# A four-layer graph kernel: the attention layer's weight passes read an fp8 copy of the adjacency, held for two pairs of tiles, in place of f32 chunks

## The reference

```python
# layer 0: attention in both signs
h = inp @ W;  Wh1 = h @ a[:F];  Wh2 = h @ a[F:]
e = leaky_relu(Wh1 + Wh2.T, 0.2)
attention = softmax(where(adj > 0, e, -1e12));  negative = -softmax(where(adj > 0, -e, -1e12))
x = x + elu(concat([attention @ inp, negative @ inp]) @ wtrans)
# layer 1: relu((d^-1/2 adj d^-1/2 @ h) @ W + b)     layer 2: relu(adj @ (h > 0) @ sign(W).T)
# layer 3: (1 - t) * (h @ W) + t * (adj @ (h @ W))
```

## Time and profile before

| | |
|---|---|
| timed runs, us | 1029.56, 1032.15, 1032.72 |
| profiled execution, us | 1028.39, of which the span 1026.8 |
| PE, DVE, ACT, POOL busy in the span | 95%, 74%, 45%, 7% |
| attention's steady part, one pair | 35.6 us stretch: PE 35.60, DVE 33.2, ACT 25.4 busy |
| DMA packets in all | 154.81 MB |

### The profile page before, as it was taken

One profiled execution on the slowest core, in us unless ns is written; L12 is line 12 of the kernel. 1 busy time (PEld: TensorE's weight loads), 2 busy tenths in 40 slices (PEclk: granted clock), 3 DMA queues, 4 the chain that ended last, 5 costly groups with the idle time before them and its releaser, 6 DMA issues.

```text
span 1026.8 us, 20940 instructions
## 1 busy us (share of the span) xinstructions
PE 974.0 (95%) x7549; PEld 708.5 (69%) x7549; DVE 760.9 (74%) x1143; ACT 457.7 (45%) x827; POOL 72.8 (7%) x148
## 2 busy tenths in 40 slices
PE   5778899999999999999999799999999999999996
PEld 4436588888888888888888355555568874555553
DVE  5468889999999999999997565555557775555553
ACT  3476676777677777767767322222220001111111
POOL 2000000000000000000031000000004320000000
PEclk7589899999999999999999899999999999999998
DMA  6044476666666666566664034544654445656661
GB/s 233 1 45 96 119 158 139 147 151 146 151 157 151 141 159 124 148 143 158 144 124 170 33 132 171 196 165 169 216 185 160 137 165 184 208 201 209 215 220 61
DMA packets 44045, 154.81 MB, mean 151 GB/s; under 512 B 5068, under 2 KB 25189, under 8 KB 43877
## 3 DMA queue, kind: packets, MB, share of 16 engines
q1 hardware_dynamic: 35285, 142.37, 40.7%
q0 software_dynamic: 7488, 11.08, 13.3%
q10 hardware_dynamic: 1232, 0.85, 0.3%
HBM read 173.02 MB, written 14.50 MB: 183 GB/s over the span
## 4 chain that ended last, share of the span: by engine, by line
PE 45%; DVE 31%; issue 12%; ACT 8%; DMA 2%; DVEq 1%; ACTq 0%; POOL 0%; POOLq 0%
PE f_ya L1247 35%; DVE f_wm L1428 9%; DVE f_gb L1429 7%; DVE f_s_mat L1432 6%; PE f_yb L1164 5%; ACT f_gb L953 4%; DVE f_s_mat L1437 2%; ACT f_s_mat L963 2%; PE f_ya L1135 1%; PE f_yb L1158 1%; DVE f_xs L1467 1%; DVE f_w_res L1465 1%; DVE f_yt_sb L1457 1%; DMA f_ident<-ident_dram 1%; DMA f_e_tile<-f_e_dram 1%
## 5 line engine op out<-in xcount | busy, mean ns | idle before, releaser
L1174 PE MATMUL f_ya<-f_x_mat,f_s_mat 128*128 128x257 f16 x2028 | 351.3, 272 | 4.8 <-DVE f_s_mat L1437 4.8
L1174 PE MATMUL f_yb<-f_x_mat,f_s_mat 128*128 128x257 f16 x2028 | 334.2, 273 | 0.0
L1247 PE MATMUL f_ya<-f_x_mat,f_a 128*128 128x512 f16 x1352 | 318.7, 382 | 4.7 <-DVE f_x_mat L1495 4.7
L1247 PEld LDWEIGHTS f_ya<-f_x_mat,f_a 128*128 128x128 fp8e4 x1352 | 132.2, 99 | 140.1 <-DVE f_x_mat L1495 5.2
L1174 PEld LDWEIGHTS f_yb<-f_x_mat,f_s_mat 128*128 128x128 f16 x2028 | 196.1, 97 | 28.7
L1174 PEld LDWEIGHTS f_ya<-f_x_mat,f_s_mat 128*128 128x128 f16 x2028 | 149.7, 97 | 23.8 <-issue 5.3
L953 ACT ACTIVATE f_gb<-f_e_tile,f_expc 128x256 f32<-128x256 f32 x338 | 139.8, 493 | 3.2 <-DVE f_s_mat L1437 2.3
L963 ACT ACTIVATE f_s_mat<-f_wm 128x1792 f16<-128x1792 f32 (+1 forms) x52 | 82.7, 1590 | 111.1 <-DVE f_wm L1428 104.8
L1177 PE MATMUL f_ya<-f_ones,f_a 128*128 128x1 f16 x676 | 111.8, 165 | 0.0
L1428 DVE TENSOR_TENSOR f_wm<-f_gb,f_a 128x1792 f32<-128x1792 f32 (+1 forms) x52 | 98.2, 1888 | 14.9 <-ACT f_gb L953 13.1
L1571 DVE SCALAR_TENSOR_TENSOR f_gb<-f_gb 128x1664 f32<-128x1664 f32 x52 | 98.0, 1886 | 11.9 <-DVE f_s_mat L1621 11.9
(11 more groups left out here) (138 smaller groups left out, 745.8 us busy)
## 6 DMA issues: line engine op xcount, KB each, us to landing
f_gb<-adj_dram SPq DMA_DIRECT2D x52, 832.0 KB, 4.9
f_a<-f_a_dram SPq DMA_DIRECT2D x39, 832.0 KB, 4.5
f_a<-adj_t_dram SPq DMA_DIRECT2D x26, 896.0 KB, 6.1
f_a<-adj_t_dram SPq DMA_DIRECT2D x26, 768.0 KB, 5.1
f_a<-adj_t_dram POOLq DMA_DIRECT2D x26, 224.0 KB, 5.8
f_a_dram<-f_a SPq DMA_DIRECT2D x26, 224.0 KB, 6.1
f_a<-adj_t_dram POOLq DMA_DIRECT2D x26, 192.0 KB, 4.6
f_a_dram<-f_a SPq DMA_DIRECT2D x26, 192.0 KB, 5.9
```

The source lines that it names most:

```text
L1174: return pe.matmul(bank[:, 0:F + 1], s_mat[:, j, side, i], x_mat[:, j, x_side, 0:F + 1], start=start, stop=stop)
L1247: return pe.matmul(bank_a[p][:, 0:W], a8_pair[:, r, at:at + P], x_layer[layer][:, j, 0:W], start=(j == 0), stop=(j == TILES - 1))
```

## The change

`a8` becomes two pairs deep, `[P, 2, TILES, HP]`, and DVE's two passes read it in place of `a32`. The buffer `a32`, its 52 loads on SP and their semaphores go. POOL's loads no longer wait for `et_done` (the scores); from pair 2 on they wait for PE and DVE to be through the same chunk two pairs before, and for its store. The later layers read their pairs from the same two buffers, which turns the parity `r0` round and splits what SP waits for at the hand-over.

```diff
-        a32 = sb("a32", [P, 2, CM * HP])
-        a8 = sb("a8", [P, TILES, HP], F8)
+        a8 = sb("a8", [P, 2, TILES, HP], F8)
-        a8_pair = a32[:].rearrange("p r c -> p (r c)").bitcast(F8)[:, 0:2 * TILES * HP].rearrange("p (r c) -> p r c", r=2)
+        a8_pair = a8[:].rearrange("p r j c -> p r (j c)")
...
-                def load_chunk(m, c):
-                    lo, hi = CHUNKS[c]
-                    sp.dma_start(blocks(a32, c), adj_t[bass.ds(m, 1), :, lo:hi, :].rearrange("a p j c -> p (a j) c"))\
-                      .then_inc(a_here[c % 2], 16)
...
                 def pair(m, r, k):
-                    start = isinstance(m, int) and m == 0
+                    if isinstance(m, int) and m == 0:
+                        wait(et_done, 2)
+                        sp.dma_start(e_dram, e_rows[:]).then_inc(e_stored, 16)
+                        wait(e_stored, 16)
+                        load_e(0, 0)
+                        load_e(1, 1)
                     for c in range(NC):
-                        n = NC * m + c
-                        if not (start and c < 2):
-                            wait(wp_done, n - 1)
-                        load_chunk(m, c)
...
-                        elif not start and c == 1 and not (isinstance(m, int) and m == PAIRS - 1):
+                        if c == 1 and not (isinstance(m, int) and m in (0, PAIRS - 1)):
                             wait(g_done, NC * m)
                             load_e(m + 1, 1 - r)
-                        if not (start and c < 2):
-                            store_a8(m if c >= 2 else m - 1, (c - 2) % NC)
+                        store_a8(m, r, k, c)
...
-                wait(wp_done, NC * PAIRS)
-                for c in range(NC):
-                    wait(a8_stored[c], 16 * PAIRS)
-                wait(lo_done, 2 * NC * PAIRS)
...
-                    r0 = layer % 2 ^ 1
+                    r0 = layer % 2
                     if layer > 1:
                         wait(mm_done[layer - 1], TILES - 2)
+                    else:
+                        for c in range(NC):
+                            wait(a8_stored[1, c], 16 * (PAIRS // 2))
                     load_pair(layer, 0, r0)
                     if layer > 1:
                         wait(mm_done[layer - 1], TILES)
+                    else:
+                        for c in range(NC):
+                            wait(a8_stored[0, c], 16 * (PAIRS // 2 + 1))
+                        wait(s_free, NC * PAIRS)
+                        wait(lo_done, 2 * NC * PAIRS)
                     load_pair(layer, 1, r0 ^ 1)
...
                 def load_a8(m, c):
-                    if not isinstance(m, int) or m > 0:
-                        g.wait_ge(s_free, NC * m + c - NC + 1)
+                    if m > 1:
+                        g.wait_ge(s_free, NC * (m - 2) + c + 1)
+                        g.wait_ge(wp_done, NC * (m - 2) + c + 1)
-                        g.wait_ge(a8_stored[c], 16 * m)
+                        g.wait_ge(a8_stored[m % 2, c], 16 * (m // 2))
-                    g.dma_start(a8[:, lo:hi, :], adj_t[m, :, lo:hi, :])\
+                    g.dma_start(a8[:, m % 2, lo:hi, :], adj_t[m, :, lo:hi, :])\
-                g.wait_ge(et_done, 2)
...
-                def produce(m, c):
+                def produce(m, r, k, c):
-                    v.wait_ge(a_here[c % 2], 16 * (2 * m + c // 2 + 1))
+                    v.wait_ge(a8_here[r, c], 16 * k + 16)
-                    v.tensor_tensor(part(wm, c), part(gb, c), part(a32, c), ALU.min).then_inc(wm_done, 1)
-                    v.scalar_tensor_tensor(part(gb, c), part(gb, c), 1.0, part(a32, c), ALU.max, ALU.mult).then_inc(wp_done, 1)
+                    v.tensor_tensor(part(wm, c), part(gb, c), a8_part(r, c), ALU.min).then_inc(wm_done, 1)
+                    v.scalar_tensor_tensor(part(gb, c), part(gb, c), 1.0, a8_part(r, c), ALU.max, ALU.mult).then_inc(wp_done, 1)
```

More of the change, by code:

```diff
@@ L618, in fast_program @@
         xlo = sem("xlo")
-        a_here = [sem(f"a_here{i}") for i in range(2)]
         e_here = [sem(f"e_here{i}") for i in range(2)]
-        a8_stored = [sem(f"a8_stored{c}") for c in range(NC)]
+        a8_stored = {(r, c): sem(f"a8_stored{r}{c}") for r in range(2) for c in range(NC)}
         g_done = sem("g_done")
@@ L627, in fast_program @@
         hp_done = sem("hp_done")
-        a8_here = [sem(f"a8_here{c}") for c in range(NC)]
+        a8_here = {(r, c): sem(f"a8_here{r}{c}") for r in range(2) for c in range(NC)}
         check_here = [sem(f"check_here{i}") for i in range(2)]
@@ L692, in part, with a8_part @@
             return buffer[:, c % 2, 0:(hi - lo) * HP]
+        def a8_part(r, c):
+            lo, hi = CHUNKS[c]
+            return a8_pair[:, r, lo * HP:hi * HP]
         def blocks(buffer, c):
@@ L731, in load_e, with store_a8 @@
                       .then_inc(e_here[r], 16)
-                def store_a8(m, c):
+                def store_a8(m, r, k, c):
                     lo, hi = CHUNKS[c]
-                    wait(a8_here[c], 16 * (m + 1))
+                    wait(a8_here[r, c], 16 * k + 16)
                     sp.dma_start(a8_dram[bass.ds(m, 1), :, lo * HP:hi * HP].rearrange("a p c -> p (a c)"),
-                                 a8[:, lo:hi, :].rearrange("p j c -> p (j c)").bitcast(U8)).then_inc(a8_stored[c], 16)
+                                 a8[:, r, lo:hi, :].rearrange("p j c -> p (j c)").bitcast(U8)).then_inc(a8_stored[r, c], 16)
                 def pair(m, r, k):
-                    start = isinstance(m, int) and m == 0
-                    for c in range(NC):
-                        n = NC * m + c
-                        if not (start and c < 2):
-                            wait(wp_done, n - 1)
-                        load_chunk(m, c)
-                        if start and c == 1:
-                            wait(et_done, 2)
-                            sp.dma_start(e_dram, e_rows[:]).then_inc(e_stored, 16)
-                            wait(e_stored, 16)
-                            load_e(0, 0)
-                            load_e(1, 1)
-                        elif not start and c == 1 and not (isinstance(m, int) and m == PAIRS - 1):
+                    if isinstance(m, int) and m == 0:
[4 more added lines that the diff above has]
+                        load_e(1, 1)
+                    for c in range(NC):
+                        if c == 1 and not (isinstance(m, int) and m in (0, PAIRS - 1)):
                             wait(g_done, NC * m)
                             load_e(m + 1, 1 - r)
-                        if not (start and c < 2):
-                            store_a8(m if c >= 2 else m - 1, (c - 2) % NC)
+                        store_a8(m, r, k, c)
                 all_pairs(sp, pair)
-                for c in (2, 3):
-                    store_a8(PAIRS - 1, c)
                 wait(s_free, NC * (PAIRS - 1) + 1)
@@ L1176, in main_block @@
                         add(ya[s, p], 0, 0, start=(j == 0))
-                        pe.matmul(ya[s, p][:, F + 1:F + 2], a8[:, j, i], ones16[:, 0:1], start=False,
+                        pe.matmul(ya[s, p][:, F + 1:F + 2], a8[:, s, j, i], ones16[:, 0:1], start=False,
                                   stop=(j == TILES - 1), skip_group_check=True)
@@ L1194, in pair @@
                             pe.wait_ge(lo_done, 2 * n + 2)
-                            pe.wait_ge(a8_here[c], 16 * m + 16)
+                            pe.wait_ge(a8_here[s, c], 16 * k + 16)
                         if c == 0 and (not known or m > 1):
@@ L1503, in first_pair @@
                     x0_low(1)
-                    produce(0, 0)
-                    produce(0, 1)
+                    produce(0, 0, 0, 0)
+                    produce(0, 0, 0, 1)
                     x0_low(2)
-                    produce(0, 2)
+                    produce(0, 0, 0, 2)
                     v.wait_ge(late_here, 32)
@@ L1510, in first_pair @@
                     v.tensor_scalar(omt_scaled[:], t_col[:], -1.0 / SCALE, 1.0 / SCALE, ALU.mult, ALU.add).then_inc(wready, 1)
-                    produce(0, 3)
+                    produce(0, 0, 0, 3)
                     x0_low(3)
@@ L1521, in pair @@
                             divisors(m - 1, 1 - r)
-                        produce(m, c)
+                        produce(m, r, k, c)
                         if not known or m > 1:
```

3 lines of the change are left out of this document (2 added, 1 removed).

## The result

| | before | after |
|---|---|---|
| timed runs | 13 | 13 |
| median, us | 1029.47 | 1025.06 |
| lowest to highest, us | 1026.57 to 1032.72 | 1023.58 to 1026.54 |
| profiled execution, us (span) | 1028.39 (1026.8) | 1026.46 (1024.8) |

A forecast was written before the change was run, and what follows sets the result against it. PE was taken to bound the steady attention part at 35.86 us a pair, with DVE ahead. All terms were 0 except -0.8 us for the early loads: 1032.15 - 0.8 = 1031.3 us, range 1027.5 to 1034.5.

The forecast's parts named there:

- The loads that go: SP's queue in the attention layer: about 43 MB of f32 loads vanish, nothing on the chain waits for them; 0 us.
- the passes on fp8: DVE's 104 passes reading an 8-bit operand in place of f32: neither faster nor slower; 0 us.
- the new wait: DVE now waits for POOL's fp8 loads, which land with 31 us to spare, so it is never taken; 0 us.
- the hand-over's DMAs: Passage to layer 1: second pair and check loads move behind PE's end, with 8 us to spare; 0 us.
- The early loads: Start: POOL's eight fp8 loads finish before the scores' store, so the scores reach ACT sooner; -0.8 us, or 0 if overlapping.
- Rival B: Start: one or both of PE's lower-clock stretches at 75 to 90 and 105 to 122 us go; 1027.4 us, chance 12%.
- What bounds the kernel: Attention layer: PE sets the pace at 35.86 us a pair; DVE, at 35.60, leads by 8.9 us at the narrowest, growing.
- The forecast's own warning: Sign of being wrong: time moved by over 3 us with all expected trace signs in place would point to the clock.

The follow-up runs named there:

- Run 3: Changed kernel with the 52 f32 loads put back on SP at their old places, read by nobody: 1025.06 us (0.9949 to the kernel before).
- run 10: Kernel before with early fp8 loads and its f32 loads counted by eight semaphores, so DVE waits for 16k + 16; operand stays f32: 1024.90 us (0.9949).
- run 2: Kernel before, f32 loads kept, with only POOL's wait for the scores before its first four fp8 loads taken out: 1026.60 us (0.9966).
- run 5: Kernel before, with POOL's first four fp8 loads made to wait until both row-score loads have landed: 1026.78 us (0.9964).
- run 6: Changed kernel with one more long-met wait on DVE in each of its 52 chunks: 1027.88 us (0.9980 to the kernel before).
- run 11: Kernel before with the eight semaphores and DVE's wait for 16k + 16 alone, without early loads: 1029.83 us (0.9996).
- run 7: Changed kernel with DVE's two long-met waits moved behind the two passes of the chunk before: 1022.00 us (0.9917 to the kernel before).
- run 12: run 7 with PE's two idle stretches of the start filled with 36 and 38 matmuls nobody reads: 1019.13 us (0.9897 to the kernel before).
- run 1: Changed kernel with POOL's first eight fp8 loads waiting for the scores again: 1029.33 us (0.9996 to the kernel before).

## Why the prediction was wrong, step by step

**The loads that go, the passes on fp8, the new wait, the hand-over's DMAs: right.** Each was put at 0. Run 3 (traffic back: no change) and run 10 (f32 operand and buffer: the changed kernel's time) show it to within their intervals, and no wait for a load appears.

**The early loads: the mechanism was right, the term was mis-sized.** The step says "only 63.06 - 62.17 = 0.89 us can be had", and then takes 0.8 from the median, 1032.15. That cap belongs to one execution of 1028.39, in which ACT was free at 62.17, 0.9 to 1.4 us later than in the other crowded profiles, so that most of the load's 8.3 us was over. Taking the chain's 7.46 us for the whole load hid this. The term is 3.6 us by run 2 and 3.9 by run 5. It is made of ACT's wait, 0.9 to 3.2 us, and, where that is long, of 1.3 us that PE loses at the lower clock from 68 us on. "Rival B" looked for the clock's share in the stretches at 75 and 105, which stay in the changed kernel (0.83 from 65 to 85, and 0.80 from 105 to 122); the one that goes is at 68, and the profile of before that I had does not contain it.

**What bounds the kernel: wrong at one end.** The step that failed is "Nothing that happens on DVE, ACT, SP or in the DMA engines in that stretch moves the end unless it uses up the lead." It holds for PE in the steady part. But at the hand-over PE waits 4.70 us for DVE's x, and DVE gets there by its own chain through all 13 pairs. The prediction had that row and called it "a chain of arithmetic that has no DMA in it": true, and beside the point. What a pair costs DVE comes out there once for each pair that has it, eleven times in run 6 (0.25 and 2.74 us). The form of the wait is worth 0.08 to 0.09 us in the looped pairs, and the idle time at the hand-over is 0.77 us shorter for it (run 10 against run 2). Behind that, from where PE resumes to the end of the span, run 2 takes 1026.0 - 581.78 = 444.2 us and run 10 1024.2 - 580.69 = 443.5. The 0.7 us may be the stretch from 845 to 865 us, granted 0.91 in all three profiles of before and in runs 2 and 5, and 1.00 in after, run 10 and run 11. But runs 7 and 12 have 0.91 and 0.92 there and are the fastest, so the form of the wait does not decide it, and what does stays open.

**The sum as measured.** By the ratios the early loads are worth 3.5 us (run 2), early loads and form together 5.3 (run 10, 3.4 to 7.1), and the change measured 4.2 (2.9 to 5.6). The two terms cover the change. The second is shown by the traces, 0.8 us at the hand-over; in the medians it is not clear of the noise, neither here nor in run 11.

**The medians.** The forecast's own warning, "a time moved by over 3 us with all of these in place, which would point to the clock", sent the first look to the clock. The crowded profiles show that it was the transfer first and the clock behind it.

## What to carry to other kernels

A wait that ends with a DMA has a spread, and one profile shows one draw of it: before a gain is capped by what the chain shows, compare the profiled execution with the median of the runs, and read the transfer's own landing time where other queues share its engines (9.2 us against 3.6); the chain cuts that time where the waiting engine came free. An engine with a lead in the steady state is off the path only until the stage ends; where the next stage waits for it, each instruction of its sequencer that nothing hides counts once a loop, and waits long met belong behind queued work. Before an instruction is added or moved to test a gap, look up in which chunk the gap is. Idle time of the matrix engine shortly before a full stretch cost twice here, once for itself and once at the lower clock, and filling it with matmuls that nobody reads paid.

## What the runs showed of the hardware

- A wait that is long met is not always free on DVE: one more in each chunk cost 0.11 and 0.14 us in two of four chunks and nothing in the other two, before one of which the engine waits for ACT anyway, 0.25 us a pair (run 6); two waits moved behind queued work gave back 0.26 us a pair (run 7).
- Two 128 KB loads beside 0.85 MB of converting loads of POOL's queue (1.22 MB in run 1) landed 9.2 to 10.0 us after their issue, and 3.2 to 4.1 us where POOL's loads stood before or after them.
- 44 MB of loads beside a steady part in which PE has no gap cost nothing that shows, neither in time (0.9949 with them, 0.9933 to 0.9966, and 0.9959 without) nor in the granted clock of the steady part, 1.00 with both.
